# Counts of edges in ranges of at most 20 nodes, two PSUM banks for counts and two for the sums of the tensor pass

## The reference

```
# 0: tensor product network; w = silu(edge_in @ W1) @ W2 for every edge
mid = [w1*y0[src]*ea0, w4*dot(y1[src], ea1), (w2*y0[src])*ea1, w3*y1[src]*ea0]
agg = segment_sum(mid, dst)                    # then two linear maps
# 1: gated messages and a GRU
agg = segment_sum((x[src] @ Wm + bm) * sigmoid(x[src]@a1 + x[dst]@a2 + b), dst)
# 2: two sort layers: the first 4 neighbours of each node, sorted per feature,
#    weighted; missing ones filled; a*x added; batch norm; residual
out = sum_m sort(first4(x[src]))[m] * cw[m] + cb + a*x
# 3: four mean-aggregating layers (width 128, 256, 256, 128) with batch norm and relu
z = (segment_sum(z[src], dst) / count) @ Wl.T + bl + z @ Wr.T
```

## Time and profile before

| | |
|---|---|
| median of 3 runs | 4152.91 us (4146.51 to 4159.01) |
| the profiled execution | 4154.11 us, of which the span from first to last instruction 4152.2 us |
| busy: PE, DVE, ACT, POOL | 3219.9, 2353.6, 1233.5, 2723.6 us |
| mean granted TensorE clock | 0.866 of full speed |

### The profile page before, as it was taken

How to read it: one execution, slowest core, us unless ns; L and a number is a source line. 1 busy time by engine, 2 the same in 40 slices (tenths; PEclk the granted TensorE clock), 3 DMA queues, 4 the chain that set the end, 5 groups by cost and what they waited for, 6 DMA issues and landing times. The chain is left out here.

```text
span 4152.2 us, 70522 instructions
## 1 busy us (share of the span) xinstructions
PE 3219.9 (78%) x23509; PEld 2310.3 (56%) x23621; DVE 2353.6 (57%) x7895; ACT 1233.5 (30%) x2805; POOL 2723.6 (66%) x2731
## 2 busy tenths in 40 slices
PE   2688788788878888755544457996999889997997
PEld 2577676666646565533322244664666666775554
DVE  5688788888845677566667672236233333334223
ACT  1333344444524455344322340003111131112112
POOL 1777777777624777457747756653777667775774
PEclk8799999999989999875555568998999999998998
DMA  5432445666754555313344548982999769996996
GB/s 180 111 82 70 99 100 105 118 122 127 124 145 125 128 140 135 81 41 81 81 93 82 111 90 279 282 256 99 307 301 301 245 234 298 309 300 214 294 291 187
DMA packets 522641, 702.45 MB, mean 169 GB/s; under 512 B 70731, under 2 KB 415858, under 8 KB 521382
## 3 DMA queue, kind: packets, MB, share of 16 engines
q1 hardware_dynamic: 414630, 435.93, 38.5%
q0 software_dynamic: 107648, 261.94, 22.6%
HBM read 579.08 MB, written 118.51 MB: 168 GB/s over the span
## 5 line engine op out<-in xcount | busy, mean ns | idle before, releaser
L1786 POOL DMA_INDIRECT pass_rows<-table_sage,src_idx x1040 | 998.0, 960 | 367.7 <-issue 294.0
L1189 POOL DMA_INDIRECT pass_rows<-table_tensor,src_idx x784 | 775.4, 989 | 279.4 <-issue 231.9
L1845 PE MATMUL pass_dense_ps<-x 128*128 128x512 f16 x3528 | 604.7, 328 | 28.4 <-DMA x<-table_sage 26.9
L2770 POOL DMA_INDIRECT sort_rows<-table_sort,slot_idx x392 | 399.6, 1019 | 171.2 <-issue 116.4
L1845 PE MATMUL pass_dense_ps<-rb 128*128 128x512 f16 x2646 | 466.4, 331 | 31.3 <-DMA rb<-table_sage 27.2
L1845 PEld LDWEIGHTS pass_dense_ps<-x 128*128 128x128 bf16 x3528 | 336.0, 98 | 242.0 <-DMA x<-table_sage 28.7
L1432 POOL DMA_INDIRECT pass_rows<-table_gate,src_idx x314 | 332.5, 1059 | 159.8 <-issue 91.5
L1272 PE MATMUL pass_sums_ps<-pass_hot,pass_prod_a 128*128 128x128 f32 x1568 | 240.2, 301 | 167.0 <-DVE rb L1289 165.7
L1845 PEld LDWEIGHTS pass_dense_ps<-rb 128*128 128x128 bf16 x2646 | 229.2, 98 | 236.5 <-DMA rb<-table_sage 33.0
L1916 DVE TENSOR_TENSOR pass_scaled_sums<-pass_sums_ps,rc 128x52 f32<-128x52 f32 (+16 forms) x316 | 57.2, 222 | 517.8 <-PE pass_sums_ps L1879 480.1
L1272 PEld LDWEIGHTS pass_sums_ps<-pass_hot,pass_prod_a 128*128 128x128 f32 x1568 | 211.2, 208 | 213.2 <-DVE rb L1289 199.7
(11 more groups left out here) (391 smaller groups left out, 6403.0 us busy)
## 6 DMA issues: line engine op xcount, KB each, us to landing
rb<-dense SPq DMA_DIRECT2D x196, 288.0 KB
x<-dense SPq DMA_DIRECT2D x294, 192.0 KB
x<-table_sage SPq DMA_DIRECT2D x294, 192.0 KB
dense<-re SPq DMA_DIRECT2D x10, 3136.0 KB, 24.2
rb<-dense SPq DMA_DIRECT2D x98, 309.5 KB
pass_counts<-dense SPq DMA_DIRECT2D x147, 192.0 KB
rb<-table_sage SPq DMA_DIRECT2D x294, 96.0 KB
dense<-x SPq DMA_DIRECT2D x6, 3136.0 KB, 26.3
```

Of the source, the lines that this page charges most:

```text
L1189: nc.gpsimd.indirect_dma_start(rows[:, h, t, :], None, table, bass.IndirectOffsetOnAxis(ap=idx[:, at:at + 1], axis=0)).then_inc(gathered[h ...
L1786: nc.gpsimd.indirect_dma_start(rows[:, h, t, :], None, table, bass.IndirectOffsetOnAxis(ap=idx[:, at:at + 1], axis=0)).then_inc(gathered[h ...
L1845: ins = nc.tensor.matmul(dense_ps[:, a * bank_cols + at:a * bank_cols + to], table_ring[:, k, from_table:from_table + P], counts_ring[:, k ...
L2770: nc.gpsimd.indirect_dma_start(rows[:, b, j, :], None, table, bass.IndirectOffsetOnAxis(ap=slot_idx[:, at:at + 1], axis=0)).then_inc(gathe ...
```

## The change

Ranges are planned with at most 20 nodes in both shares (30 and 34 before), and a range may now have a single tile (an assertion against it goes). From the kernel's own constants:

| | ranges | of one tile | compared keys, all tiles | matmul pieces of tiles | runs |
|---|---|---|---|---|---|
| first share, before | 138 | 0 | 458,738 | 1136 | 13 |
| first share, after | 217 | 107 (tiles 361 to 467) | 354,662 | 886 + 107 | 13 |
| second share, before | 54 | 0 | 154,056 | 340 | 3 + 4 |
| second share, after | 108 | 108 (all) | 89,964 | 216 + 107 | 4 + 4 |

A range then has at most 49 x 20 = 980 columns and takes two PSUM banks instead of three. In a range of one tile the column of the range before is written first and starts the accumulation of its 49 columns, so the tile's product is cut at 49. The bank that is free goes to the sums of the tensor pass: they use two banks by turns, and TensorE waits for the addition before the last instead of the last. The table of positions gets entries of its own for the starts of runs (`run_offset`), since with one-tile ranges the old place is taken. Small tensors are merged.

```diff
-NEAR_ENDS, NEAR_WIDTHS = windows_of(0, HOT_TILES, 30)
-LATE_ENDS, LATE_WIDTHS = windows_of(HOT_TILES, DENSE_TILES, 34)
+NEAR_ENDS, NEAR_WIDTHS = windows_of(0, HOT_TILES, 20)
+LATE_ENDS, LATE_WIDTHS = windows_of(HOT_TILES, DENSE_TILES, 20)
...
-assert min(b - a for a, b in zip(HOT_CUTS, HOT_CUTS[1:])) > 1
-assert MOST_TILES * P <= 2048 and KEYS <= 4 * 512
+assert MOST_TILES * P <= 2048 and KEYS <= 2 * 512
...
+def run_offset(share, run):
+
+    return DENSE_TILES + share * len(SHARES[0][5]) + run
...
-        sums = s.ps("sums", [P, 512])
+        sums = s.ps("sums", [P, 2, 512])
...
-                    if holds_back(q * n_acc):
-                        pe.wait_ge(added, q * n_acc)
+                    if holds_back((q - 1) * n_acc):
+                        pe.wait_ge(added, (q - 1) * n_acc)
                     pe.wait_ge(operands_made, q + 1)
                     for a, prod in enumerate((prod_a, prod_b)):
                         for t in range(GROUP_TILES):
-                            ins = nc.tensor.matmul(sums[:, a * WIN:(a + 1) * WIN], prod[:, r, t, :], hot[:, r, t, :],
+                            ins = nc.tensor.matmul(sums[:, r, a * WIN:(a + 1) * WIN], prod[:, r, t, :], hot[:, r, t, :],
...
-                                  start=False, stop=False, skip_group_check=True)
-        for at in range(0, keys, 512):
-            wide = min(512, keys - at)
-            ins = self.nc.tensor.matmul(self.counts[:, at:at + wide], self.hot_low[:, (t // G) % 2, t % G, :],
-                                        self.hot_key[r][:, at:at + wide], start=begins, stop=ends)
+                                  start=begins, stop=False, skip_group_check=not begins)
+        alone = begins and ends and w > self.windows[0]
+        cuts = [0] + [BLOCKS] * alone + [*range(512, keys, 512), keys]
+        for at, to in zip(cuts, cuts[1:]):
+            ins = self.nc.tensor.matmul(self.counts[:, at:to], self.hot_low[:, (t // G) % 2, t % G, :],
+                                        self.hot_key[r][:, at:to], start=begins and not (alone and at == 0), stop=ends)
...
-        at = self.position(SP_E, HOT_CUTS[first] + 1, self.most) if q > 0 else 0
+        at = self.position(SP_E, run_offset(self.share, q), self.most) if q > 0 else 0
```

More of the change, by code:

```diff
@@ L145 @@
 UNPAIRED = [*range(PAIRED), *range(PAIRED + COLD_GROUPS, HOT_GROUPS)]
-assert SPLIT * SPLIT_COLS * P == BASIS * EDGE_COLS and STACK <= P and BUILD_KEYS <= 3 * 512
+assert SPLIT * SPLIT_COLS * P == BASIS * EDGE_COLS and STACK <= P and BUILD_KEYS <= 2 * 512
 assert 0 <= PAIRED and PAIRED + COLD_GROUPS <= HOT_GROUPS and BLOCKS < COLD_GROUPS
-assert min(b - a for a, b in zip(HOT_CUTS, HOT_CUTS[1:])) > 1
-assert MOST_TILES * P <= 2048 and KEYS <= 4 * 512
+assert MOST_TILES * P <= 2048 and KEYS <= 2 * 512
 assert ITERS == BLOCKS and TILES * P >= N_EDGES and REGION >= N_NODES + WIN and CHUNK * CHUNKS == NP
@@ L1288, in add_up @@
                     into = cols(region, start, REACHES[q])
-                    nc.vector.tensor_tensor(into, into, sums[:, a * WIN:a * WIN + REACHES[q]], ALU.add).then_inc(added, 1)
+                    nc.vector.tensor_tensor(into, into, sums[:, q % 2, a * WIN:a * WIN + REACHES[q]], ALU.add).then_inc(added, 1)
             def keep_beside(q):
@@ L2011, in __init__ @@
     def __init__(self, nc, sb):
-        self.any, self.group = sb("far_any", [1, 1], I32), sb("far_group", [1, WINDOWS], I32)
+        found = sb("far_found", [1, 1 + WINDOWS], I32)
+        self.any, self.group = found[:, 0:1], found[:, 1:1 + WINDOWS]
         self.shift = sb("far_shift", [P, WINDOWS])
@@ L2127, in _ @@
             after(nc.vector.tensor_tensor(place, dst[:, 0:DENSE_TILES], based, ALU.subtract))
-            for _, _, node, _, _, runs in SHARES:
-                for a, _ in runs[1:]:
-                    at = HOT_CUTS[a]
-                    nc.vector.tensor_scalar(offsets[:, at + 1:at + 2], based[0:1, at:at + 1], float(-node), None, ALU.add)
+            for share, (_, _, node, _, _, runs) in enumerate(SHARES):
+                for q, (a, _) in enumerate(runs):
+                    at, to = HOT_CUTS[a], run_offset(share, q)
+                    if q > 0:
+                        nc.vector.tensor_scalar(offsets[:, to:to + 1], based[0:1, at:at + 1], float(-node), None, ALU.add)
             nc.vector.tensor_copy(low, low_part)
@@ L2159, in _ @@
             dve.wait_ge(counted, 1)
-            nc.vector.tensor_scalar(far.group[:], count_ps[0:1, 0:WINDOWS], -1.0, 0.0, ALU.add, ALU.max)
+            nc.vector.tensor_scalar(far.group, count_ps[0:1, 0:WINDOWS], -1.0, 0.0, ALU.add, ALU.max)
             after(nc.vector.tensor_copy(last[:], base_ps[:, 0:WINDOWS]))
@@ L2167, in _ @@
             after(nc.vector.reduce_max(top[:], most_ps[:, 0:P], mybir.AxisListType.X))
-            nc.vector.tensor_scalar(far.any[:], top[:], -0.5, None, ALU.is_ge)
+            nc.vector.tensor_scalar(far.any, top[:], -0.5, None, ALU.is_ge)
         @block.tensor
@@ L2606, in __init__ @@
     def __init__(self, nc, s, share, part, key, low, offsets, same, iota, dense, stages, stored, room=None):
+        self.share = share
         self.key_from, _, _, _, self.windows, self.runs = SHARES[share]
@@ L2928, in gnn_kernel @@
         bases = sb("bases", [1, GROUPS + 2], I32)
-        offsets = sb("offsets", [1, DENSE_TILES], I32)
+        offsets = sb("offsets", [1, DENSE_TILES + sum(len(share[5]) for share in SHARES)], I32)
         iota, ident = sb("iota", [P, WIN]), sb("ident", [P, P])
-        ones, eps = sb("ones", [P, P]), sb("eps", [P, 1])
+        ones, small = sb("ones", [P, P]), sb("small", [P, 5])
+        eps, scale, shift = small[:, 0:1], small[:, 1:3], small[:, 3:5]
         inv_cols = sb("inv_cols", [P, BLOCKS])
         slot_idx = sb("slot_idx", [P, BLOCKS * SLOTS], I32)
-        scale, shift = sb("scale", [P, 2]), sb("shift", [P, 2])
         stats = sb("stats", [P, BLOCKS * 6])
@@ L2947, in _ @@
                 nc.vector.memset(X[:, NP:REGION], 0.0)
-                nc.vector.memset(eps[:], EPS)
+                nc.vector.memset(eps, EPS)
                 nc.vector.memset(rel[:, TILES:], -1.0)
```

## The result

The changed kernel takes 4179.7 us (median of 5 runs, 4178.1 to 4188.1) where the kernel before took 4152.9: ratio 1.007, 95% interval 1.0054 to 1.0086. On a second chip it was 1.0053 (1.0041 to 1.0065). It is slower, and both intervals are clear of 1. The time lies inside the range for 8 in 10 and outside the forecast's own.

What follows compares the result with a forecast made beforehand. GpSimd's gathers, their releases by TensorE's sums, or a slower new chain were taken to set the pace. Terms -4 - 4 + 15 - 6 = +1 gave 4155, as median 4154 us; own range 4142 to 4166, 8 in 10 4130 to 4184.

Steps and rivals of the forecast that it cites:

- The chain of one-tile ranges: Tensor pass from tile 361: TensorE and ACT alternate per range, 2.21 us each, 5.5 us per turn taken; +15 us.
- Rival 1: Late tensor pass: alternation of TensorE and ACT exposed, 6.2 us per turn; +46 in place of +15, 4186 us; chance 0.28.
- a load costs little while TensorE is still busy: Late tensor pass: with two register loads of a turn hidden, 5.3 us per group instead of 6.2.
- my bound for "wrong": Late tensor pass, 900 us on: above 6.2 us per group, or as fast as before, would refute the forecast.
- The gathers' stretch: Tensor pass: less comparing on DVE shortens GpSimd's gathers; -4 us, bounds -8 and 0.
- before tile 361 this only adds slack, and I count nothing: Tensor pass before tile 361: narrower tiles save TensorE about 0.12 us each, counted as no gain.
- The sort stages: Both sort stages: chains hide behind gathers, gathers' stretch shrinks with the comparisons; -6 us, from 9 us to 0.
- The second bank: Tensor pass: sums start 0.33 us sooner, counting only where GpSimd waits for them; -4 us, at most 7.6, at least 0.
- rival 3: Tensor pass: second bank also removes GpSimd's 44.9 us of waits; 4113 us; chance 0.03.
- After the sort stages: After 2431 us: counted 0 (+-5); any change there beyond 5 us would show the forecast wrong.
- The clock: Late tensor pass: TensorE's granted clock clearly below 0.92 would show the forecast wrong, since matmuls were priced at that.

## Why the prediction was wrong in size and right in mechanism

**The chain of one-tile ranges, +15 us, is the step that failed.** It measured +35.0 us, over the last 192 gathers, with 5.2 us that the gathers themselves gave back already taken off. Its links were right: 0.05 + 0.45, 0.49, 0.43 and 0.79 were priced, 0.49, 0.55, 0.42 and 0.74 to 0.93 came out, and 2.21 us per range became 2.2 to 2.4. Rival 1's turns of two and three ranges (5.2 and 7.4 us) came to 5.10 and 6.86 away from stores. What failed is the sentence "a load costs little while TensorE is still busy", with 5.5 us per turn taken from it. The 0.08 of the earlier trace rows is the load of a range's second tile. It starts at 1095.6, while the first tile's matmuls run (1095.46 to 1096.18), and takes 0.30 us there as anywhere:

```profile
L2638 PEldq TENSOR_LOAD <-offsets x1: 297/297/297, 1095.6 to 1095.6; - x1
```

A range of one tile has no first tile, so the load stands bare between the wait and the matmul, as the same text's own "behind that wait in TensorE's order" says. It was bare 61 times on TensorE, and ACT idled before 100 copies.

The second part of the error was in no case of the prediction, though the trace of the kernel before had loads of 0.98 us. In the first 6 us behind a store's issue, a handover with a load takes 1.04 to 1.12 at the median. The eight turns of two or three ranges at a store took 7.45 and 8.88 in place of 5.10 and 6.86, (4 x 2.35 + 4 x 2.02) / 40 = 0.44 us over the 40 turns. Without that the late turn would be 5.95 (an estimate). It is 6.39, and 6.42 by the gathers: above rival 1's 6.2 and above my bound for "wrong". With both loads ahead, a turn at a store is no longer than another. The Trainium skill (DMA: Bandwidth & Descriptors, "Latency and other measured facts") has about 600 ns as a floor for such a load. The loads here take 0.30 and 0.28 us at the median, under that floor (handovers with and without one differ by 0.36 and 0.30), and up to 0.99 behind a store.

**The gathers' stretch, -4 us**, was too small: -11.8, beyond its bound of -8. The comparisons fell by 28.7 of the 33 us predicted, so it is 0.41 us of gathers per us of comparison if they do it all, above the 0.16 that the prediction took from the rows as a limit. But in the sort stages 17.3 us of comparisons went and the gathers gave 1.3. The gain comes with the first share's ranges: the gathers of the pass take 774.5 to 777.4 us in the three kernels with wide ranges there and 763.5 to 768.6 in the others. Whether through comparisons or through something else that goes with the narrow ranges was not tried. And "before tile 361 this only adds slack, and I count nothing" was wrong as well: GpSimd's waits for sums fell by 9.4 us there.

**The sort stages, -6 us**, gave -3.6, and not by the way that was priced. From the first sort gather to the first gather of the next stage it is 642.1 us in place of 645.7. The gathers gave nothing: 1019 ns became 1016 in place of 1003, and in all kernels they take 394.5 to 399.6 us with wide ranges and 394.6 to 401.1 with narrow ones. Between the two stages there are 44.7 us from gather to gather where there were 41.3 (44.7 to 47.8 in all kernels with narrow ranges, 41.3 to 42.7 in those with wide ones). The first stage's last store is issued 7.0 us behind its last gather, before 3.1; whether that makes it was not tried. Behind the last gather of all, though, it takes 82.4 us to the next stage's first in place of 88.2 (81.6 to 82.5 and 88.2 to 92.5 in all kernels). In the kernel before, TensorE still has four tiles of up to 1568 columns to do there, in the changed kernel one of 882; the prediction looked at the gathers alone.

**The second bank, -4 us.** The argument against the 161.6 us wait of the earlier trace rows held: 152 us are still there, and rival 3 is out. Of the 4 us nothing can be told.

**After the sort stages** the shift went from +21.7 to +24 us, within the 5 allowed. **The clock**, which the text named as a way to be wrong, fell to 0.88. The idle matmuls show that it isn't the main cause.

The sum by what was measured: the pass starts 0.7 us later, then -15.1 and +35.0 in it, +4.1 between its last gather and the gate stage's first, +0.5 to the sort stages, -3.6 in them, +2.3 behind them: +24. That the time lies in the range for 8 in 10 is in part luck. The pass gave back 15 us before the one-tile ranges where 8 were counted for all of it; with those 8 it would be about 4187 us (an estimate), outside. Rival 1 had 4186 and 0.28; it named the mechanism, the place and the point from which it decides. I put it below the forecast on the strength of one row of another kind of range.

## What to carry to other kernels

When ranges get so small that each needs one handover from engine to engine, list what stands between the wait and the first useful instruction in each engine's order. A register load there is 0.3 to 0.4 us on the path each time, and 1 us near a store; issue it ahead of the wait. A row that shows a cost hidden speaks only for places with the same neighbour in front: look for what hides it before you take the price over. One link out of a chain of two engines may give most of what both give (0.9946 and 0.9989 against 0.9951), so neither of the single trials tells the share of its link.

## What the runs showed of the hardware

- A register load takes 0.30 us on TensorE and 0.28 on ACT (median of 323 and 305), and up to 0.96 and 0.99 in the first microseconds behind the issue of a 3.1 MB store. A handover between ACT and TensorE takes 0.12 to 0.14 us with the load ahead of the wait, 0.42 on ACT and 0.49 on TensorE with the load behind it, and 1.0 to 1.2 near a store. Twice the bytes don't stretch that, though the DMA engines are then 0.97 busy late in the pass. What in those 6 us slows the load stays open.
- SyncE issues a 3.1 MB store in 0.41 us, a second one right behind it in 15.6 to 19.2, and the next, small DMA in up to 26. What else hangs on that queue comes late: 64 us more of waits for edge terms in one kernel.
- "issue" as the end of a wait held two handovers and a copy of another engine in one case (3.03 us), and a wait for staging on ACT in another (11.03 us). It says that no releaser was found, not that the engine was busy issuing.
- The granted clock late in the pass fell from 0.92 to 0.87 when TensorE had gaps of 1 to 2 us in most turns. It came back to 0.91 with 12 idle matmuls in some of them, and the ratio stayed at 1.0045 (1.0025 to 1.0065).
